# Slot order of the first attention: scores two tiles ahead, exponential ahead of the FiLM copies, weight folding last on TensorE

## The chip, the cores and the metric

The kernel runs on one core of a Trainium2 chip. The metric is the device time of one execution in microseconds (us), lower is better. The engines are TensorE (PE, with PEld for its weight loads), VectorE (DVE), ScalarE (ACT), GpSimd (POOL) and SyncE (SP, which here only issues DMAs). Each engine runs its own instruction stream in order; engines meet at semaphores.

## The reference, cut to what matters

The whole program is two layers, each an attention and a mixture of experts; the change is confined to the first attention and to the work that is run beside it. For every token the first attention keeps the 32 largest of 64 scores per head, takes a softmax over them, averages over four heads, and makes from the result a scale and a shift (FiLM) for the normalised token:

```python
Q = (x_text @ Wq).reshape(Bb, Tt, H, DH)
K = (x_vision @ Wk).reshape(Bb, Gg, H, DH)
scores = jnp.einsum('bthd,bghd->bhtg', Q, K) / np.sqrt(DH)
topv, topi = jax.lax.top_k(scores, K_TOP)          # 32 of 64
probs = jax.nn.softmax(topv, axis=-1)
attn_mean = attn.mean(axis=1)                      # over the 4 heads
c_t = jnp.einsum('btg,bgd->btd', attn_mean, V)
scale_in, shift_in = jnp.split(c_t @ W_film_in + b_film_in, 2, axis=-1)
x = x * (1.0 + mod_gate * scale_in) + mod_gate * shift_in
y = s4d(x, log_dt, A_re, A_im, C_re, C_im, D_skip)
```

Two things that later stages need are made in the same stage: the convolution kernel of `s4d` (powers of complex numbers, then a Toeplitz layout in memory), and the expert weights of the last stage with their low-rank parts added (`W + A B`, transposed; called folding).

## The kernel before

The stage `first_attention` (L596 on) works on 32 tiles of 128 tokens. Every engine runs a loop of slots, `march(slot, first, last)`; in slot x each engine handles several tiles at different depths, `x.by(d)` being tile x+d. Nothing but the order of the code and the semaphores sets the order of the work. Buffers are doubled by the tile's parity (`j`).

For tile x the chain is as follows. PE turns the token and context rows (`turn`, L815 and L818), ACT copies them from PSUM (`xf`, `cf`). PE projects queries and keys (`qk`, L833 and L834), ACT copies them (`qt`, and four copies into `kb`). PE makes the scores into `pss` (L808), ACT copies them into `dd`, POOL adds the mask term and writes `sc` (L741). DVE selects in four rounds of four MAX8 (L937) and four MATCH_REPLACE8 (L950). After the first round POOL writes `sc` minus the maximum into `dd` (L737), ACT takes the exponential `ee` (L895). In the next slot DVE makes the masked product `pr` out of `work` and `ee` (L958), its sum and reciprocal (`weights`). POOL scales and adds up the heads into `at` (L748 to L754). PE turns `at` (L839), ACT copies it into the block-diagonal `abd`, PE multiplies it with the context (`vec`, L829, the wait names say u), ACT copies `us`, PE makes the FiLM rows (`film`, L825), ACT copies them (`fi`, `FO`), and POOL applies them (L759 to L762).

Beside this runs a list of 34 pieces, one a slot (`side_job`): PE makes piece x+3 in slot x (`side_piece`) into the one PSUM bank `side`, and ACT copies piece x+2 out of it in slot x (`keep_piece`). PE starts piece n only when ACT has kept piece n-1 (`side_kept`). From piece 13 on they come in threes for each expert: turn (one transpose), first (eight matmul pairs, L281 and L283), second (four pairs, L293 and L294). Piece 7 is first of expert 0 and piece 12 its second. The folded weights stand in one buffer, `fold.done`, that SP stores to memory after each second; ACT's copy of the next first waits for that store.

The order within a slot before is, on PE: score of tile x+1, turn x+3, film x-3, vec x-2, qk x+2, side piece, turn of `at` x-1. On ACT: score copy x+1, turn copies x+3, `us` x-2, kept piece, normalised tile, exponential x, `qt` and `kb` x+2, FiLM copies x-3, `abd` x-1. POOL has, besides its part of the chain, products of complex powers in slots 1 to 4 (`kernel_part`, K.more of 4 at once in slot 4), `fold_norm` in slot 0 and the second normalisation of eight tiles in every eighth slot.

Of the kernel before, what the change touches and what calls it, by code (L numbers as in the profile page):

```python
# [11 lines left out]
ALU = mybir.AluOpType  # L12
# [3 lines left out]
P = 128  # L16
# [198 lines left out]
class Fold:  # L215
# [9 lines left out]
    def __init__(self, C, A, G, ctx):  # L225
        self.A, self.G = A, G
        NC = self.NC

        def sb(name, shape, n):
            return [C.sb(f"fold_{name}{j}", shape, ctx=ctx) for j in range(n)]  # L230

        self.wr, self.w2r = sb("wr", [P, 2, NC, D], self.DEPTH), sb("w2r", [D, HE], self.DEPTH)
        self.br, self.b2r = (C.sb("fold_" + n, [P, NE, k], ctx=ctx) for n, k in (("br", P), ("b2r", 32)))
        self.ar, self.a2 = C.sb("fold_ar", [P, NE, D], ctx=ctx), C.sb("fold_a2", [P, NE // 4, HE], ctx=ctx)
        self.bt, self.bt2 = sb("bt", [P, P], 2), C.sb("fold_bt2", [P, NE // 4, P], ctx=ctx)
        self.done = C.sb("fold_done", [P, 2 * NC * P + NC * D], ctx=ctx)

    def semaphores(self, C):
        self.factors, self.added, self.stored = (C.sem("fold_" + n) for n in ("factors", "added", "stored"))
        self.loaded = [C.sem(f"fold_loaded{j}") for j in range(self.DEPTH)]  # L240
# [22 lines left out]
    def store(self, sp, e):  # L263
        sp.dma_start(self.G.folded[e, :, 0:2 * self.NC * P + self.NC * D], self.done[:]).then_inc(self.stored, 16)
# [38 lines left out]
    def keep_first(self, act, bank, e):  # L303
        after(act, self.stored, 16 * e)
        return act.activation(self.done[:, 0:2 * self.NC * P], bank[:, 0:2 * self.NC * P], ACT.Copy)

    def keep_weights(self, act, bank, e):
        n = 2 * self.NC * P
        return act.activation(self.done[:, n:n + self.NC * D], bank[:, 0:self.NC * D], ACT.Copy)
# [12 lines left out]
class Kernel:  # L322
# [263 lines left out]
def first_attention(nc, C, A, G):  # L586
# [4 lines left out]
    with ExitStack() as ctx:  # L591
        def two(name, shape):
# [5 lines left out]
        sc, wk_, m8 = two("sc", [P, H0, T]), two("work", [P, H0, T]), two("m8", [P, H0, 4, 8])  # L598
        dd, ee, pr = two("dd", [P, H0, T]), two("ee", [P, H0, T]), two("pr", [P, H0, T])
# [11 lines left out]
            "turned", "turned_sb", "qk", "qk_sb", "scores", "scores_kept", "scores_sb", "max", "diff", "exp",  # L611
# [25 lines left out]
        with nc.Block() as block:  # L637
# [5 lines left out]
            def _(sp):  # L643
# [31 lines left out]
                march(slot, -3, NT + 2)  # L675
                sp.wait_ge(s["toeplitz"], 16 * 4)
                sp.wait_ge(fold.stored, 16 * NE)

            @block.gpsimd
            def _(pool):  # L680
# [17 lines left out]
                def kernel_part(t):  # L698

                    U, z1 = K.U, K.one(K.V, 1)  # L700
                    if t == 1:
                        step.then(pool.tensor_scalar(K.t[:, 0, :], z1[0], -1.0, None, ALU.add))
                        K.times(step, pool, K.one(U, 0), (K.t[:, 0, :], z1[1]), K.Q, K.tu)
                    if t == 2:
                        pool.wait_ge(s["powers"], 2)
                        K.more(step, pool, U, 1, K.z[8], K.tu)
                    if t == 3:
                        K.more(step, pool, U, 2, K.z[16], K.tu)
# [20 lines left out]
                def slot(x):  # L729
                    j, a, c, m, n = x.j, x.by(3), x.by(-4), x.by(-1), x.by(1)  # L730
                    if x.t == 0:
                        fold_norm()
                    if x.real() and x.t % 8 == 0:
                        second_norm(slice(x.t, x.t + 8))
# [4 lines left out]
                    if n.real():  # L739
                        pool.wait_ge(s["scores_kept"], n.t + 1)  # L740
                        pool.tensor_tensor(sc[n.j][:], dd[n.j][:], wide(G.pen[:, n.t:n.t + 1, :], [P, H0, T]),  # L741
                                           ALU.add).then_inc(s["scores_sb"], 1)
                        pool.wait_ge(s["scores_sb"], n.t + 1)
# [19 lines left out]
                    if c.real():  # L763
                        pool.wait_ge(s["mod"], c.t + 1)
                    kernel_part(x.t)

                march(slot, -3, NT + 4)

            @block.tensor
            def _(pe):  # L770
                def side_piece(n):
                    name, e = side_job(n)
# [28 lines left out]
                def slot(x):  # L801
                    turn, qk, score, attn, vec, film = (x.by(d) for d in (3, 2, 1, -1, -2, -3))
# [38 lines left out]
                march(slot, -3, NT + 3)  # L841

            @block.scalar
            def _(act):
# [30 lines left out]
                def slot(x):  # L875
                    turn, qk, attn, vec, film, score, n = (x.by(d) for d in (3, 2, -1, -2, -3, 1, KEPT))
                    if score.real():
                        act.wait_ge(s["scores"], score.t + 1)
                        copy(dd[score.j][:].rearrange("p h g -> p (h g)"), pss[score.j][:, 0:H0 * T]).then_inc(s["scores_kept"], 1)
                    if turn.real():  # L880
# [4 lines left out]
                        copy(cf[j][:], psa[j][0:DC, P:2 * P]).then_inc(s["turned_sb"], 1)  # L885
                    if vec.real():
                        act.wait_ge(s["u"], vec.t + 1)
                        copy(us[vec.j][0:DC, :], psb[vec.j][0:DC, P:2 * P]).then_inc(s["u_sb"], 1)
                    keep_piece(x.t + 2)
                    if x.real() and n.real():  # L890
                        act.activation(G.XT[:, n.t, :], G.X[:, n.t, :], ACT.Identity, scale=norm["rstd"][:, n.t:n.t + 1],
                                       bias=norm["shift"][:, n.t:n.t + 1]).then_inc(s["normal"], 1)
                    if x.real():
                        act.wait_ge(s["diff"], x.t + 1)
                        act.activation(ee[x.j][:], dd[x.j][:], ACT.Exp, scale=scale).then_inc(s["exp"], 1)  # L895
# [9 lines left out]
                    if film.real():  # L905
                        act.wait_ge(s["film"], film.t + 1)
                        after(act, s["mod"], film.t - 1)
                        copy(fi[film.j][:], psf[:, 0:256])
                        copy(G.FO[:, film.t, :], psf[:, 256:512]).then_inc(s["film_sb"], 1)
# [6 lines left out]
                march(slot, -3, NT + 3)  # L916

            @block.vector
            def _(dve):
# [11 lines left out]
                def top(x, r, src, ready):  # L931

                    marks = []
                    for h in range(H0):
                        if r > 0:
                            own.wait(ready[h])
# [7 lines left out]
                def replace(x, r, src, h, found):  # L944
# [5 lines left out]
                    return own.did(dve.match_replace(wk_[x.j][:, h, :], m8[x.j][:, h, r, :], src[:, h, :], TAKEN))  # L950
# [1634 lines left out]
```

## Time and profile before

| | |
|---|---|
| time, median of three runs (lowest, highest) | 938.17 us (937.61, 940.75) |
| span of the profiled execution | 935.4 us |
| busy share of the span: PE, DVE, ACT, POOL | 76%, 72%, 51%, 60% |
| first attention, from the first MAX8 to the last masked product | 33.04 to 247.75 us |
| DVE waiting for the exponential in it | 21.0 us in 12 waits |
| mean granted TensorE clock from 94 to 248 us | 0.74 of full speed |

The profile is of one execution; its span is from the first to the last instruction. The granted clock is the share of full speed at which TensorE was allowed to run; 1.00 and 0.50 are its two levels of 2.4 and 1.2 GHz. A timeline row gives the start, the duration, the engine, the line of the kernel, the operation and its operands, and in square brackets the idle time of the engine just ahead of it with what ended it.

### The profile page before, as it was taken

What the parts mean: (1) busy time and instruction counts of PE and PEld (TensorE: products, weight loads), DVE (VectorE), ACT (ScalarE), POOL (GpSimd) and SP (SyncE); (2) the same over time, 40 slices, a digit from 0 to 9 for tenths busy, and PEclk for the clock granted to TensorE, in tenths of its full rate; (3) what the DMA queues carried; (4) which work ended last, traced back from release to release, by engine and by line L of the source; (5) the groups of instructions that cost most, each with busy time, mean ns of one, the idle gap of its engine ahead of it and who ended that gap; (6) DMA issues with size and microseconds to landing.
All of it is one profiled execution on the core that took longest, in us unless ns stands there. A gap on an engine that the chain in (4) does not pass through costs nothing. (4 is left out here: it accounts for less than half of the span.)

```text
span 935.4 us, 20537 instructions
## 1 busy us (share of the span) xinstructions
PE 710.3 (76%) x6072; PEld 508.4 (54%) x6072; DVE 673.2 (72%) x3212; ACT 473.4 (51%) x1318; POOL 564.8 (60%) x931
## 2 busy tenths in 40 slices
PE   0686898979883999972498528998888874799970
PEld 0353554545483656631275426766666652699970
DVE  6898989978524688769111167598998887699974
ACT  3566576735200455450133175577777761577740
POOL 7688877766526544210677667345777767277770
PEclk9767787957555999996599855798988885899995
DMA  6300112997213977700365330000000002698928
GB/s 143 57 25 10 41 45 64 86 88 96 40 45 140 290 250 257 243 23 0 39 115 132 88 137 1 2 4 13 25 26 25 25 28 76 216 279 264 260 69 270
DMA packets 98829, 94.41 MB, mean 101 GB/s; under 512 B 37511, under 2 KB 82302, under 8 KB 98142
## 3 DMA queue, kind: packets, MB, share of 16 engines
q1 hardware_dynamic: 91268, 79.34, 33.1%
q0 software_dynamic: 6592, 13.58, 6.0%
q8 instruction: 50, 0.82, 0.4%
q14 instruction: 61, 0.50, 0.3%
q10 hardware_dynamic: 858, 0.17, 0.1%
HBM read 47.76 MB, written 43.19 MB: 97 GB/s over the span
## 5 line engine op out<-in xcount | busy, mean ns | idle before, releaser
L2402 POOL DMA_INDIRECT expert_pairs<-e_ys,e_home x78 | 75.4, 967 | 38.4 <-issue 23.5
L1742 POOL TENSOR_SCALAR a_kb<-a_kr,a_m,a_bk 128x128 f32<-128x128 f32 x128 | 57.9, 452 | 44.4 <-ACT a_kr L1981 32.3
L1760 POOL DMA_INDIRECT expert_slots<-r_rows,r_slotu x64 | 63.3, 989 | 30.3 <-DVE r_rows L2136 15.1
L950 DVE MATCH_REPLACE8 work<-m,work 128x64 f32<-128x64 f32 x384 | 75.7, 207 | 0.0
L1484 POOL DMA_INDIRECT ex_rows<-rows,slot_source x32 | 30.7, 960 | 52.7 <-POOLq L1163 43.2
L937 DVE MAX8 m<-work 128x8 f32<-128x64 f32 x384 | 57.0, 209 | 0.0
L825 PE MATMUL psf<-filmw,us 97*128 97x512 f32 x64 | 51.6, 902 | 3.0 <-ACT FO L846 2.9
L1815 PE MATMUL a_pss<-a_kb,a_qt 32*64 32x256 f32 x512 | 41.5, 463 | 13.9 <-ACT a_pp L1966 11.7
L2168 DVE TENSOR_REDUCE a_mx<-a_pss 128x8 f32<-128x512 f32 x64 | 43.9, 686 | 8.1 <-PE a_pss L1815 7.8
L2369 PE MATMUL e_ps<-e_XH,e_wh 128*128 128x256 f32 x156 | 48.1, 308 | 1.5 <-DVE e_XL L2414 1.5
L1536 ACT ACTIVATE ex_hs<-ex_psh,vec 128x512 f32<-128x512 f32 x32 | 22.0, 687 | 51.2 <-PE ex_psh L1517 50.5
L2371 PE MATMUL e_ps<-e_XH,e_wl 128*128 128x256 f32 x156 | 44.6, 286 | 0.0
L2370 PE MATMUL e_ps<-e_XL,e_wh 128*128 128x256 f32 x156 | 44.6, 286 | 0.0
L1961 ACT ACTIVATE a_pp<-a_dd 128x512 f32<-128x512 f32 x32 | 20.2, 631 | 45.1 <-DVE a_dd L2177 45.1
L1890 PE MATMUL a_psp<-ident,a_pp 128*128 128x128 f32 x256 | 39.5, 306 | 1.9 <-ACT a_pt L2014 1.9
L2219 DVE RECIPROCAL a_rt<-a_pso 128x128 f32<-128x128 f32 x31 | 29.5, 951 | 14.8 <-PE a_pso L1882 11.9
L1309 ACT ACTIVATE rt_rs<-mlp_psh,vec 128x512 f32<-128x512 f32 x32 | 22.0, 687 | 34.7 <-PE mlp_psh L1267 34.7
L203 POOL TENSOR_SCALAR mlp_ln_v<-mlp_ln_mv 128x4 f32<-128x4 f32 x24 | 5.5, 229 | 54.0 <-DVE mlp_ln_mv L195 54.0
L1494 POOL DMA_INDIRECT planes<-ex_ys,slot_home x32 | 31.2, 976 | 10.9 <-issue 9.1
L2177 DVE TENSOR_TENSOR a_dd<-a_mx,a_pss 128x512 f32<-128x512 f32 x64 | 35.5, 554 | 2.2
L808 PE MATMUL pss<-kb,qt 128*64 128x256 f32 x128 | 28.9, 541 | 10.7 <-ACT kb L846 10.7
L2014 ACT ACTIVATE a_pt<-a_psp 128x512 f32<-128x512 f32 x64 | 35.4, 611 | 2.2 <-PE a_psp L1890 2.0
(464 smaller groups left out, 2418.2 us busy)
## 6 DMA issues: line engine op xcount, KB each, us to landing
expert_slots<-rt_unfilled SPq DMA_DIRECT2D x151, 130.0 KB, 2.6
ahead<-folded_weights SPq DMA_DIRECT2D x20, 386.0 KB
e_wf<-folded_weights SPq DMA_DIRECT2D x19, 386.0 KB, 4.2
planes<-rt_zeros SPq DMA_DIRECT2D x4, 1024.0 KB
ew<-in_L_ffn_ew SPq DMA_DIRECT2D x16, 256.0 KB, 4.0
pair_y<-expert_pairs SPq DMA_DIRECT2D x16, 256.0 KB, 5.6
e_xr<-expert_slots SPq DMA_DIRECT2D x27, 130.0 KB, 3.3
folded_weights<-fold_done SPq DMA_DIRECT2D x8, 384.0 KB, 4.3
```

The lines of the kernel that those rows point to most:

```text
L825: pe.matmul(psf[:], us[j][:], G.filmw[:], start=True, stop=True).then_inc(s["film"], 1)
L937: mx = dve.max(m8[x.j][:, h, r, :], src[:, h, :])
L950: return own.did(dve.match_replace(wk_[x.j][:, h, :], m8[x.j][:, h, r, :], src[:, h, :], TAKEN))
L1742: m = pool.tensor_scalar(kb[a.j][:, :, h, :], k, m4[:, h:h + 1], bk4[:, h:h + 1], ALU.mult, ALU.add)
L1760: pool.indirect_dma_start(G.slots, bass.IndirectOffsetOnAxis(ap=slot[:, b, k, t:t + 1], axis=0), rb[b % NB][:, k, t, :], None).then_inc(se ...
L1815: mm = pe.matmul(pss[half][T * b:T * b + T, h, 0:HG * T], qt[g.j][rows, T * b:T * b + T], kb[g.j][rows, b, :, :], start=True, stop=True)
L1890: mm = pe.transpose(psp[half][:, k, :], pp[x.j][:, h:h + 2, :].rearrange("p h k -> p (h k)"), G.ident[:])
L2168: dve.tensor_reduce(m, scores(half), AX.X, ALU.min).then_inc(s["lowest"], 1)
L2369: pe.matmul(psh[m][c][:], wh[j][:, m, c, :], XH[j][:], start=True, stop=False)
L2370: pe.matmul(psh[m][c][:], wh[j][:, m, c, :], XL[j][:], start=False, stop=False)
L2371: pe.matmul(psh[m][c][:], wl[j][:, m, c, :], XH[j][:], start=False, stop=True).then_inc(h_ps[m][c], 1)
L2402: pool.indirect_dma_start(G.pair, bass.IndirectOffsetOnAxis(ap=home[i % NY][:, k:k + 1], axis=0), ys[i % NY][:, k, :], None).then_inc(kept ...
```

## The change

On PE every tile is turned, projected and scored one slot earlier than before (turn x+4, qk x+3, score x+2), and the side piece moves from ahead of the turn of `at` to the end of the slot. ACT's order becomes: score copy x+2 (into a buffer of its own, `raw`), turn copies x+4, exponential x, FiLM copies x-3, `us` x-2, `qt` and `kb` x+3, kept piece, normalised tile, `abd` x-1. POOL adds the mask two tiles ahead, and for that waits until DVE has read the buffer it writes over (`replaced`, a new semaphore, which the last MATCH_REPLACE8 of the first round raises). `fold.done` is doubled, with one store semaphore for each half. POOL's products start two slots earlier, the largest is split over slots 2 and 3, `fold_norm` moves to the end of slot 1, and the second normalisation is split into four tiles in each of two slots. SP's loop starts at slot -2 and not at -3, its order within a slot is as before.

```diff
     def keep_first(self, act, bank, e):
-        after(act, self.stored, 16 * e)
-        return act.activation(self.done[:, 0:2 * self.NC * P], bank[:, 0:2 * self.NC * P], ACT.Copy)
+        after(act, self.stored[e % 2], 16 * (e // 2))
+        return act.activation(self.done[e % 2][:, 0:2 * self.NC * P], bank[:, 0:2 * self.NC * P], ACT.Copy)
...
+    def half_of_more(self, step, eng, z, a, factor, room, part):
+        by = tuple(wide(q.unsqueeze(1), [P, a, NS]) for q in factor)
+        u, out = self.powers(z, 0, a), self.powers(z, a, a)[part]
+        t0, t1 = (room[:, k, 0:a, :] for k in range(2))
+        eng.tensor_tensor(t0, u[0], by[part], ALU.mult)
+        step.then(eng.tensor_tensor(t1, u[1], by[1 - part], ALU.mult))
+        step.then(eng.tensor_tensor(out, t0, t1, ALU.add if part else ALU.subtract))
...
-                march(slot, -3, NT + 2)
+                march(slot, -2, NT + 2)
...
-                    if t == 4:
-                        K.more(step, pool, U, 4, K.z[32], K.tu)
+                    if t in (2, 3):
+                        K.half_of_more(step, pool, U, 4, K.z[32], K.tu, t - 2)
...
-                    j, a, c, m, n = x.j, x.by(3), x.by(-4), x.by(-1), x.by(1)
+                    j, a, c, m, n = x.j, x.by(4), x.by(-4), x.by(-1), x.by(2)
...
-                        pool.tensor_tensor(sc[n.j][:], dd[n.j][:], wide(G.pen[:, n.t:n.t + 1, :], [P, H0, T]),
+                        if x.real():
+                            pool.wait_ge(s["replaced"], x.t + 1)
+                            pool.wait_ge(s["diff"], x.t + 1)
+                        pool.tensor_tensor(sc[n.j][:], raw[n.j][:], wide(G.pen[:, n.t:n.t + 1, :], [P, H0, T]),
...
-                    turn, qk, score, attn, vec, film = (x.by(d) for d in (3, 2, 1, -1, -2, -3))
+                    turn, qk, score, attn, vec, film = (x.by(d) for d in (4, 3, 2, -1, -2, -3))
...
-                    side_piece(x.t + 3)
                     if attn.real():
                         pe.wait_ge(s["attn"], attn.t + 1)
                         after(pe, s["u_sb"], attn.t - 1)
                         pe.transpose(psb[attn.j][:, 0:P], at[attn.j][:], G.ident[:]).then_inc(s["attn_turned"], 1)
+                    side_piece(x.t + 3)
```

ACT in one slot of the middle of the stage, before (from the score copy on; `fold_done` is the kept side piece, here a first):

```order
L846 ACTIVATE dd<-pss 128x256 [waits att0_scores]
L846 ACTIVATE xf<-psa 128x128 [waits att0_ctx_kept,att0_turned]
L846 ACTIVATE cf<-psa 96x128
L846 ACTIVATE us<-psb 96x128 [waits att0_u]
L305 ACTIVATE fold_done<-side 128x512 [waits fold_stored,att0_side]
L891 ACTIVATE XT<-X,FO 128x128
L895 ACTIVATE ee<-dd 128x256 [waits att0_diff]
L846 ACTIVATE qt<-psa 128x128 [waits att0_scores,att0_qk]
L846 ACTIVATE kb<-psa 32x2x64 x4
L846 ACTIVATE fi<-psf 128x256 [waits att0_mod,att0_film]
L846 ACTIVATE FO<-psf 128x256
```

The same slot of ACT now:

```order
L861 ACTIVATE raw<-pss 128x256 [waits att0_scores_sb,att0_scores]
L861 ACTIVATE xf<-psa 128x128 [waits att0_ctx_kept,att0_turned]
L861 ACTIVATE cf<-psa 96x128
L904 ACTIVATE ee<-dd 128x256 [waits att0_diff]
L861 ACTIVATE fi<-psf 128x256 [waits att0_mod,att0_film]
L861 ACTIVATE FO<-psf 128x256
L861 ACTIVATE us<-psb 96x128 [waits att0_u]
L861 ACTIVATE qt<-psa 128x128 [waits att0_scores,att0_qk]
L861 ACTIVATE kb<-psa 32x2x64 x4
L306 ACTIVATE fold_done<-side 128x512 [waits fold_stored0,att0_side]
```

The exponential moved from behind `us` and the kept piece to right behind the turn copies; the kept piece moved from ahead of the exponential to behind `qt` and `kb`.

PE at the end of a slot and the start of the next, before (L273 is the side piece, a turn; L839 turns `at`; L808 opens the next slot):

```order
L833 MATMUL psa<-xf,wq 128x128 [waits att0_turned_sb]
L834 MATMUL psa<-cf,wk 128x128
L273 MATMUL side<-ident,fold_br 128x128 [waits att0_side_kept]
L839 MATMUL psb<-ident,at 128x128 [waits att0_u_sb,att0_attn]
L808 MATMUL pss<-kb,qt 64x256 [waits att0_scores_kept,att0_qk_sb]
```

The same place of PE now:

```order
L848 MATMUL psa<-xf,wq 128x128 [waits att0_turned_sb]
L849 MATMUL psa<-cf,wk 128x128
L853 MATMUL psb<-ident,at 128x128 [waits att0_u_sb,att0_attn]
L274 MATMUL side<-ident,fold_br 128x128 [waits att0_side_kept]
L823 MATMUL pss<-kb,qt 64x256 [waits att0_scores_kept,att0_qk_sb]
```

The side piece stands between the turn of `at` and the next slot's scores, with the same wait for the kept piece as before.

## Rows read from the trace of the kernel before

**Rows 1.** The page's first line.
```profile
span 935.4 us, 20537 instructions
```

**Rows 2.** Waits, 34 to 250 us: us in total, times, longest.
```profile
ACT us L846 <- PE psb L829: 35.8, 29, 2.0
...
DVE pr L958 <- ACT ee L895: 21.0, 12, 3.6
```

**Rows 3.** Timeline of DVE: the masked products of tiles 0, 9, 10, 24, 30.
```profile
40.50 0.48 DVE L958 SCALAR_TENSOR_TENSOR pr<-work,ee 128x256 f32<-128x256 f32 x1 [2.25 <-ACT ee L895]
...
99.58 0.43 DVE L958 SCALAR_TENSOR_TENSOR pr<-work,ee 128x256 f32<-128x256 f32 x1
...
105.66 0.68 DVE L958 SCALAR_TENSOR_TENSOR pr<-work,ee 128x256 f32<-128x256 f32 x1
...
198.58 0.43 DVE L958 SCALAR_TENSOR_TENSOR pr<-work,ee 128x256 f32<-128x256 f32 x1 [3.55 <-ACT ee L895]
...
241.62 0.43 DVE L958 SCALAR_TENSOR_TENSOR pr<-work,ee 128x256 f32<-128x256 f32 x1 [2.10 <-ACT ee L895]
```

**Rows 4.** Timeline, PE and ACT in one slot at clock 1.00.
```profile
177.06 0.65 PE L808 MATMUL pss<-kb,qt 128*64 128x256 f32 x4
...
178.39 0.27 ACT L846 ACTIVATE cf<-psa 96x128 f32<-96x128 f32 x1
...
179.22 0.39 PE L834 MATMUL psa<-cf,wk 96*128 96x128 f32 x2
...
180.02 0.41 ACT L895 ACTIVATE ee<-dd 128x256 f32<-128x256 f32 x1
...
180.48 1.09 ACT L846 ACTIVATE kb<-psa 32x128 f32<-32x128 f32 x4
...
181.60 0.38 ACT L846 ACTIVATE fi<-psf 128x256 f32<-128x256 f32 x1
...
181.88 0.38 ACT L846 ACTIVATE FO<-psf 128x256 f32<-128x256 f32 x1
```

**Rows 5.** Timeline, PE and ACT in one slot at clock 0.50.
```profile
201.59 1.12 PE L808 MATMUL pss<-kb,qt 128*64 128x256 f32 x4
...
205.50 0.27 ACT L846 ACTIVATE us<-psb 96x128 f32<-96x128 f32 x1 [1.70 <-PE psb L829]
...
205.68 0.63 PE L834 MATMUL psa<-cf,wk 96*128 96x128 f32 x2
...
205.94 0.41 ACT L895 ACTIVATE ee<-dd 128x256 f32<-128x256 f32 x1
...
207.67 1.12 PE L808 MATMUL pss<-kb,qt 128*64 128x256 f32 x4 [0.89 <-ACT kb L846]
```

**Rows 6.** Timeline of PE: a first from beginning to end at clock 1.00, then 0.50.
```profile
184.26 0.49 PE L281 MATMUL side<-ident,fold_wr 128*128 128x128 f32 x2
...
187.59 0.47 PE L839 MATMUL psb<-ident,at 128*128 128x128 f32 x1
...
230.86 0.68 PE L281 MATMUL side<-ident,fold_wr 128*128 128x128 f32 x2
...
236.52 0.47 PE L839 MATMUL psb<-ident,at 128*128 128x128 f32 x1
```

**Rows 7.** Windows: length, busy PE, PEld, DVE, ACT, POOL, then clock, DMA share, GB/s.
```profile
94.00:248.00 154.00, 132.57 (x511) 78.81 (x511) 137.16 (x1173) 90.05 (x343) 110.41 (x240) 0.74 0.54 67
...
104.00:106.00 2.00, 0.00 (x0) 0.00 (x0) 1.87 (x16) 1.94 (x8) 1.76 (x4) 0.90 0.00 1
```

**Rows 8.** Timeline of ACT: the kept first that waited for a store.
```profile
197.64 0.60 ACT L305 ACTIVATE fold_done<-side 128x512 f32<-128x512 f32 x1 [5.47 <-DMA folded_weights<-fold_done]
```

**Rows 9.** Timeline of POOL: K.more in slot 4, its first instruction and what follows its six.
```profile
66.37 0.72 POOL L314 TENSOR_TENSOR toe<-toe 128x256 f32<-128x256 f32 x1
...
71.05 0.62 POOL L737 TENSOR_TENSOR dd<-sc,m 128x256 f32<-128x256 f32 x1 [0.18 <-POOL toe L319]
```

**Rows 10.** Instructions on the context rows `cs`: time from issue to landing of their loads.
```profile
DMA to landing us min/median/max: 1.7/1.8/14.8
```

More of the change, by code:

```diff
@@ L263, in store @@
     def store(self, sp, e):
-        sp.dma_start(self.G.folded[e, :, 0:2 * self.NC * P + self.NC * D], self.done[:]).then_inc(self.stored, 16)
+        sp.dma_start(self.G.folded[e, :, 0:2 * self.NC * P + self.NC * D], self.done[e % 2][:]).then_inc(self.stored[e % 2], 16)
     def turn_second(self, pe, bank):
@@ L762, in slot @@
                         pool.tensor_tensor(G.XM[:, c.t, :], xn[:], fi[c.j][:, D:2 * D], ALU.add).then_inc(s["mod"], 1)
-                    if c.real():
                         pool.wait_ge(s["mod"], c.t + 1)
                     kernel_part(x.t)
-                march(slot, -3, NT + 4)
+                    if x.t == 1:
+                        fold_norm()
+                    if x.real() and x.t % 8 in (0, 1):
+                        at_once = 8 * (x.t // 8) + 4 * (x.t % 8)
+                        second_norm(slice(at_once, at_once + 4))
+                march(slot, -4, NT + 4)
             @block.tensor
@@ L875, in slot @@
                 def slot(x):
-                    turn, qk, attn, vec, film, score, n = (x.by(d) for d in (3, 2, -1, -2, -3, 1, KEPT))
+                    turn, qk, attn, vec, film, score, n = (x.by(d) for d in (4, 3, -1, -2, -3, 2, KEPT))
                     if score.real():
                         act.wait_ge(s["scores"], score.t + 1)
-                        copy(dd[score.j][:].rearrange("p h g -> p (h g)"), pss[score.j][:, 0:H0 * T]).then_inc(s["scores_kept"], 1)
+                        after(act, s["scores_sb"], score.t - 1)
+                        copy(raw[score.j][:].rearrange("p h g -> p (h g)"), pss[score.j][:, 0:H0 * T]).then_inc(s["scores_kept"], 1)
                     if turn.real():
@@ L885, in slot @@
                         copy(cf[j][:], psa[j][0:DC, P:2 * P]).then_inc(s["turned_sb"], 1)
+                    if x.real():
+                        act.wait_ge(s["diff"], x.t + 1)
+                        act.activation(ee[x.j][:], dd[x.j][:], ACT.Exp, scale=scale).then_inc(s["exp"], 1)
+                    if film.real():
+                        act.wait_ge(s["film"], film.t + 1)
+                        after(act, s["mod"], film.t - 1)
+                        copy(fi[film.j][:], psf[:, 0:256])
+                        copy(G.FO[:, film.t, :], psf[:, 256:512]).then_inc(s["film_sb"], 1)
                     if vec.real():
@@ L904, in slot @@
                         m.then_inc(s["qk_sb"], 1)
[L905 to L909, printed above, removed]
+                    keep_piece(x.t + 2)
+                    if x.real() and n.real():
+                        act.activation(G.XT[:, n.t, :], G.X[:, n.t, :], ACT.Identity, scale=norm["rstd"][:, n.t:n.t + 1],
+                                       bias=norm["shift"][:, n.t:n.t + 1]).then_inc(s["normal"], 1)
                     if attn.real():
@@ L934, in top @@
                     for h in range(H0):
-                        if r > 0:
+                        if r == 1 and h == H0 - 1:
+                            dve.wait_ge(s["replaced"], x.t + 1)
+                        elif r > 0:
                             own.wait(ready[h])
@@ L949, in replace @@
                         own.wait(found[h])
-                    return own.did(dve.match_replace(wk_[x.j][:, h, :], m8[x.j][:, h, r, :], src[:, h, :], TAKEN))
+                    taken = dve.match_replace(wk_[x.j][:, h, :], m8[x.j][:, h, r, :], src[:, h, :], TAKEN)
+                    if r == 0 and h == H0 - 1:
+                        taken.then_inc(s["replaced"], 1)
+                        return None
+                    return own.did(taken)
                 def slot(x):
```

38 lines of the change are left out of this document (15 added, 23 removed).

## The prediction, made before the changed kernel was run

> **What bounds the kernel now.** I read the page's first line for the size of the whole: a span of 935.4 us [rows 1], 2.8 us below the median of the three runs, 938.17 us. I add the change that I work out for the span to that median. Only the first attention is touched, so every term is a difference inside its 215 us. I read the waits of that stage next, then DVE's timeline, then PE and ACT side by side in a slot at either clock.
>
> DVE sets the pace where nothing goes wrong. Its masked product comes once in a slot, and from tile 9 to tile 10 that takes 6.08 us [rows 3] with no wait. From tile 9 to tile 30 it takes 142.04 us for 21 slots, where 21 x 6.08 = 127.7, so 14.4 us are lost there. Nearly all that DVE waits for in the stage is the exponential, 21.0 us in 12 waits [rows 2].
>
> The exponential is late because ACT stands in front of it: ACT waits 35.8 us for PE's vec product to copy `us` [rows 2], and the kept piece and the exponential stand behind that copy. At clock 0.50 the exponential starts 205.94 - 201.59 = 4.35 us after PE began the slot's scores [rows 5]. Behind that is PE itself. At clock 0.50 its fixed part, from the scores to the end of the key projection, is 206.31 - 201.59 = 4.72 us [rows 5]; at 1.00 it is 179.61 - 177.06 = 2.55 us [rows 4]. A first adds 5.66 or 3.33 us [rows 6]. A second has half as many pairs: 2.83 or 1.67 us. A turn is one transpose like that of `at`: 0.47 us at the low clock [rows 6], and by my estimate half of that, 0.24, at the high one.
>
> So three slots (turn, first, second), which I call a round, cost DVE 18.24 us. They cost PE at clock 1.00 3 x (2.55 + 0.24) + 0.24 + 3.33 + 1.67 = 13.6 us. At 0.50 a slot with a turn takes 6.08 us [rows 5], held by `kb`; one with a first 4.72 + 0.47 + 5.66 = 10.85; one with a second 8.02; together 24.95. PE is far ahead at one clock and far behind at the other. The granted clock over 94 to 248 us is 0.74 [rows 7], which is (1 - 0.74) / 0.5 = 52% of the time at the low level. If PE's lead at the high clock were of no use later, a round would take 1 / (0.48/18.24 + 0.52/24.95) = 21.2 us; if all of it were, DVE's 18.24. Measured: 142.04 / 7 = 20.3. The two loops together thus explain the pace before, and I use the same form for the kernel after.
>
> **The change, part by part.**
>
> *The exponential ahead.* It now needs PE's scores and turns alone, not film, vec, `us` and the kept piece. At clock 1.00 the turn copies end at 178.39 + 0.27, 1.6 us after the slot's scores began [rows 4]. At 0.50 I estimate 2.2 us: the scores and transposes double, the two copies don't. Against 4.35 [rows 5], PE may fall some 2.2 us further behind before DVE waits. That is a margin, spent once as long as PE does not win it back.
>
> *Weight folding last.* The bank `side` holds one piece: PE makes piece x+3 when ACT has kept piece x+2. ACT did that right behind `us`, about when PE ended its key projection, so PE hardly waited. Now the kept piece stands behind the exponential, both FiLM copies, `us`, `qt` and four `kb` copies. The `at` transpose that PE does meanwhile covers 0.24 to 0.47 us of this. And behind the piece waits the next slot, since scores, turns, exponential and FiLM of slot x+1 all come after piece x+3 on PE. This closes a loop: scores, ACT's whole chain, kept piece, side piece, next scores.
>
> Its length at clock 1.00, from the start of the scores: 1.6 for the turn copies; 0.46 for exponential and `qt` (180.02 to 180.48); 0.28 + 0.38 for FiLM; 0.27 for `us` [rows 5]; 1.09 for `kb` [rows 4]; and the kept piece, 0.60 for a first [rows 8] and like the copies of 128 and 256 columns, 0.27 and 0.38 [rows 4], for the others, 0.42 on average. That sums to 4.50 us. The copies overlap by about 0.1 at each seam (`FO` starts 0.28 after `fi`, which lasts 0.38), which makes 4.0 at the least; I take 4.25. At 0.50 the key projection ends later than ACT's queue: 4.72 + 0.2 for `qt` + 1.09 + 0.42 = 6.45 us with the signal.
>
> A round of this loop is 3 x 4.25 + 5.24 = 18.0 us at clock 1.00, no shorter than DVE's 18.24: PE can no longer win anything back. At 0.50 it is 3 x 6.45 + 0.47 + 5.66 + 2.83 = 28.3, against 24.95. With 52% at the low clock a round takes 1 / (0.48/18.24 + 0.52/28.3) = 22.4 us.
>
> *Two buffers for the folded weights.* Once, a kept first waited 5.47 us for a store [rows 8], and DVE lost 3.55 us behind it [rows 3]. That is inside the 142.04 us, and goes. PE stood still through it at the low clock; I count it as two points of the share: 50%, a round of 1 / (0.50/18.24 + 0.50/28.3) = 22.2 us. Seven rounds are 155.3, that is 13.3 more than 142.04; less the margin of 2.2, **+11 us**.
>
> *POOL.* It is busy 110.41 us in the 25 slots between 94 and 248 us [rows 7], 4.4 of 6.08 each. The wait for `replaced` lies inside the 1.7 us that are left; nothing but POOL's own part stands behind it, and the masked scores are two tiles ahead. Cost: none, at most 1 us in the stage. In the start, tile 0's wait of 2.25 us [rows 3] goes, because `fold_norm` and the normalisation no longer stand ahead of its difference. The product of slot 4, six instructions that hold POOL for 71.05 - 66.37 = 4.7 us [rows 9], is split. But slot 1 now carries a product of half that width (2.3 to 4.7 us), `fold_norm` and four tiles' normalisation on top of its own work, and DVE may wait some 2.5 us for tile 2's exponential. Between -4 and +3 us, I take 0.
>
> *Context rows.* PE turns tile x+4, and SP issues the load of x+6 when vec of x-2 is done, as before. A load now has two slots, some 12 us, where it had three. The median landing takes 1.8 us, the longest 14.8 [rows 10], so between 0 and 3 us once; I take 0. The Toeplitz rows and stores behind it on SP's queue keep their order. Scores two tiles ahead buy nothing themselves: the only wait of DVE of any size is the exponential [rows 2].
>
> Sum: 938.2 + 11 = **949 us**.
>
> **The rivals.**
>
> *Faster: the exponential was all.* If the side loop is hidden, DVE runs at 6.08 throughout: 14.4 us of the 21 slots and 2.25 of the start go, 921.5 us. The 12 waits for the exponential speak for it, and that the whole ACT chain fits into 6.08 us at clock 1.00. It needs the high clock: the loop after equals the pace before (20.3, with the margin 20.6) at a low-clock share of 32%, and below that the change wins. The removed stand of 5.5 us at the low clock speaks for a lower share. Between 920 and 935 us.
>
> *No change.* Gain and longer loop cancel, at 25 to 37% low clock and with the start a little better: 935.5 to 941. That the exponential moves in name only, because it still waits behind PE's scores and turns, which come behind the side piece, ends here too.
>
> *Clearly slower: the clock falls.* In the loop PE stands idle in every slot, at 0.50 for 6.45 - 4.72 - 0.47 = 1.3 us and at 1.00 for about 1.4. Idle does cost clock here: PE has no instruction from 104 to 106 us, and the mean clock of that stretch is already 0.90 [rows 7], on the way from 1.00 to 0.50. With 75% of the time low a round takes 1 / (0.25/18.24 + 0.75/28.3) = 24.9 us: 174.1 for seven, +32 less 2 is 968 us. Against it: PE stood still for as long in slots before, where it waited for `at`. The Trainium skill speaks for this rival, "TensorE: Matmul & The Clock Gate", section "A second HAM failure mode: psum-queue depth-cycling": where TensorE pauses between groups of matmuls because it hands PSUM banks round, its clock swings and throughput falls even if the matmuls themselves are fast. The one bank `side` is such a hand-over; the row at 104 agrees that a pause costs clock, and no row shows yet what a pause in every slot does.
>
> **How the numbers follow.** The forecast (a low-clock share of about 40 to 62%, 941 to 960 us) gets 0.50, the fallen clock (beyond 960) 0.18, no change 0.14, faster 0.18. A measurement of this kernel can tell about 0.3%, 2.8 us, from no change. So faster is 0.18, same 0.14, slower 0.68. The range takes in the share from 75%, 968 us, down into the upper part of the faster case; the bounds of the start and of the loads lie inside. 930 to 968 leaves out about 0.1 on either side.
>
> **What will show it.** Right: PE waits for ACT's kept piece ahead of nearly every side piece (hardly any before), the round at clock 1.00 is near 18 us and at 0.50 near 28, the wait of ACT for `us` shrinks while DVE's wait for the exponential grows, most after a first at the low clock, and the wait for the store is gone. Wrong: slots of 6.08 us through the low clock, or PE's waits ahead of the side piece below 0.5 us. A mean clock above 0.84 in the stage would make it faster, one below 0.65 slower than the forecast. A POOL busy without a pause over several slots after slot 10 would refute its zero.

## The result and the profile after

The changed kernel takes **989.09 us** (median of four runs, 984.53 to 990.42) where the kernel before takes 938.89 beside it: a ratio of 1.0548, 95% interval 1.0501 to 1.0595, some 50 us slower. The forecast was 949 us with a range up to 968. The direction was right; the size was that of the third rival, "clearly slower: the clock falls", which had a chance of 0.18, and it went 21 us beyond that rival's price of 968. Where one execution of a kernel below ran far slower than its others at a clearly lower granted clock, its median is that of the others.

The page of the kernel after: first line, busy times, and the granted clock in 40 slices (each about 25 us, so the first attention is the slices 2 to 12).

```profile
span 989.2 us, 20586 instructions
...
PE 746.6 (75%) x6072; PEld 530.6 (54%) x6072; DVE 673.1 (68%) x3212; ACT 474.9 (48%) x1318; POOL 571.1 (58%) x947
...
PEclk9967765565555579999659975589988886799995
```

The span is 53.8 us above that of [rows 1], and the first attention holds nearly all of it. DVE's masked products, the marks of [rows 3], show where. These are the products of tiles 0, 9, 10 and 30, and between the last two those that bound three slots at the low clock: one with a first (149.47 to 161.65), one with a second (241.26 to 250.86) and one with a turn (250.86 to 257.76):

```profile
41.46 0.67 DVE L980 SCALAR_TENSOR_TENSOR pr<-work,ee 128x256 f32<-128x256 f32 x1 [3.01 <-ACT ee L904]
...
108.79 0.69 DVE L980 SCALAR_TENSOR_TENSOR pr<-work,ee 128x256 f32<-128x256 f32 x1 [0.71 <-ACT ee L904]
...
118.28 0.70 DVE L980 SCALAR_TENSOR_TENSOR pr<-work,ee 128x256 f32<-128x256 f32 x1 [3.28 <-ACT ee L904]
...
149.47 0.42 DVE L980 SCALAR_TENSOR_TENSOR pr<-work,ee 128x256 f32<-128x256 f32 x1 [0.95 <-ACT ee L904]
...
161.65 0.42 DVE L980 SCALAR_TENSOR_TENSOR pr<-work,ee 128x256 f32<-128x256 f32 x1 [6.23 <-ACT ee L904]
...
241.26 0.43 DVE L980 SCALAR_TENSOR_TENSOR pr<-work,ee 128x256 f32<-128x256 f32 x1 [4.96 <-ACT ee L904]
...
250.86 0.43 DVE L980 SCALAR_TENSOR_TENSOR pr<-work,ee 128x256 f32<-128x256 f32 x1 [3.66 <-ACT ee L904]
...
257.76 0.44 DVE L980 SCALAR_TENSOR_TENSOR pr<-work,ee 128x256 f32<-128x256 f32 x1 [0.96 <-ACT ee L904]
...
290.54 0.56 DVE L980 SCALAR_TENSOR_TENSOR pr<-work,ee 128x256 f32<-128x256 f32 x1
```

From tile 0 to tile 9 the stage now takes 67.33 us where it took 59.08; with tile 0 itself 0.96 later, tile 9 is 9.2 us late. From tile 9 to tile 30 it takes 181.75 us where it took 142.04, which is 39.7 more. Together tile 30 is 48.9 us late. The waits of the stage (34 to 310 us; us in total, times, longest) name the loop of the prediction:

```profile
ACT raw L861 <- PE pss L823: 83.3, 31, 6.3
POOL sc L753 <- ACT raw L861: 77.3, 22, 7.1
DVE pr L980 <- ACT ee L904: 71.0, 25, 6.2
...
PE psb L853 <- POOL at L765: 20.3, 15, 6.3
...
PE side L294 <- ACT fold_done L306: 10.5, 7, 1.8
PE side L274 <- ACT fold_done L310: 9.1, 6, 1.6
...
PE side L282 <- ACT fold_bt L302: 5.7, 6, 1.4
```

ACT no longer waits for PE's vec product [rows 2] but for PE's scores, 83.3 us: the whole slot begins late. DVE's wait for the exponential went from 21.0 us in 12 [rows 2] to 71.0 in 25. PE waits for the kept piece ahead of its side piece, 25.3 us in 19 waits, 1.33 each, about the 1.3 of the prediction. In the kernel before (34 to 250 us) it waited 8.5 us in 11 there, 5.6 of them in the one wait for the store:

```profile
PE side L293 <- ACT fold_done L305: 7.4, 5, 5.6
...
PE side L273 <- ACT fold_done L309: 1.1, 6, 0.2
```

The clock is the other part. Three windows of the kernel after: tile 0 to tile 9, tile 9 to tile 30, and 23 us inside it (length; busy PE, PEld, DVE, ACT, POOL; granted clock, DMA share, GB/s). Behind them are the same two stretches of the kernel before.

```profile
41.40:108.80 67.40, 46.19 (x180) 27.57 (x179) 54.33 (x460) 38.83 (x136) 50.84 (x108) 0.75 0.05 12
108.80:290.50 181.70, 149.03 (x463) 87.97 (x463) 125.97 (x1071) 84.34 (x318) 107.86 (x234) 0.59 0.39 57
139.00:162.00 23.00, 20.01 (x59) 11.67 (x59) 13.19 (x114) 9.52 (x36) 10.45 (x23) 0.50 0.15 41
```

```profile
40.50:99.60 59.10, 45.84 (x181) 27.07 (x181) 54.05 (x460) 38.76 (x139) 51.48 (x111) 0.68 0.06 15
99.60:241.60 142.00, 121.68 (x479) 72.43 (x479) 125.51 (x1071) 84.70 (x323) 100.73 (x218) 0.75 0.58 73
```

0.59 is (1 - 0.59) / 0.5 = 82% of the time at the low level, where the kernel before had a granted clock of 0.75, or 50%, between the same two tiles. From 139 to 162 us PE stays at the low level throughout.

### The profile page after: what moved, and what is told of

Read it like the earlier page. It is cut to its first block and busy times, and to the rows that moved or that the text cites. A ratio compares the mean times of both kernels' runs of the same rounds, so it can differ in the third digit from the quotient of the medians.

```text
span 989.2 us, 20586 instructions
## 1 busy us (share of the span) xinstructions
PE 746.6 (75%) x6072; PEld 530.6 (54%) x6072; DVE 673.1 (68%) x3212; ACT 474.9 (48%) x1318; POOL 571.1 (58%) x947
## 5 line engine op out<-in xcount | busy, mean ns | idle before, releaser
L753 POOL TENSOR_TENSOR sc<-raw,pen 128x256 f32<-128x256 f32 x32 | 23.1, 723 | 79.5 <-ACT raw L861 78.0
L980 DVE SCALAR_TENSOR_TENSOR pr<-work,ee 128x256 f32<-128x256 f32 x32 | 15.8, 494 | 71.9 <-ACT ee L904 71.0
L840 PE MATMUL psf<-filmw,us 97*128 97x512 f32 x64 | 59.7, 1034 | 1.0 <-ACT us L861 1.0
L861 ACT ACTIVATE raw<-pss 128x256 f32<-128x256 f32 x32 | 12.3, 383 | 84.5 <-PE pss L823 84.5
```

Source lines behind the costliest of these rows:

```text
L840: pe.matmul(psf[:], us[j][:], G.filmw[:], start=True, stop=True).then_inc(s["film"], 1)
```

## The experiments

The theory was: the kept piece behind ACT's whole queue and the one bank `side` close a loop through PE and ACT; PE pauses in it in every slot; and the granted clock falls with that, which makes each turn of the loop longer. The rivals were that one of the other parts (POOL's split work, the wait for `replaced`, the context loads, the exponential's new place) costs the time, and that the loop alone does so without the clock.

### The two moves of the side piece, undone one by one

The kept piece goes back to the front of ACT's queue, here right behind the exponential:

```diff
                     if x.real():
                         ... exponential ...
+                    keep_piece(x.t + 2)
                     if film.real():
...
-                    keep_piece(x.t + 2)
```

> The changed kernel with one move undone: ScalarE's copy of the side piece stands right behind the exponential again, ahead of the FiLM copies, us, qt and kb; TensorE keeps the side piece last. Theory of the side loop (the piece is kept too late, and TensorE stands in front of the bank): the wait ahead of the side pieces goes, a round (turn, first, second) at clock 0.50 falls from 27.4-28 to about 25, at 1.00 it is about 19 because the turn of at waits for POOL; 960 to 970 us. Rival, the clock fell for another reason and ScalarE's order does not matter: 985 to 990 us. Rival, TensorE's order (folding last) is to blame: 985 or more.

Measured: 951.72 us in two runs, ratio 1.0118 (1.0083 to 1.0153), which is less than any of the expectations. One line on ACT gives back 37 of the 50 us. No wait for the kept piece ahead of a side piece is left; PE now waits longer for `at`. Waits from 34 to 300 us, and the window from tile 9 to tile 30:

```profile
PE psb L853 <- POOL at L765: 38.4, 18, 6.0
...
DVE pr L980 <- ACT ee L904: 36.4, 15, 4.7
```

```profile
102.10:257.90 155.80, 136.50 (x469) 84.35 (x470) 126.79 (x1071) 85.49 (x319) 108.52 (x236) 0.62 0.52 66
```

The 13 us that stay belong to PE's other move, as the kernel with both moves back shows below: with the side piece behind the turn of `at`, PE has nothing to do while it waits for `at`. The clock is still at 0.62, yet the stretch is 26 us shorter than in the kernel after, at 0.59: a low clock without the late kept piece costs far less. How much of the 13 us is the clock is not shown.

The other move alone, the side piece back ahead of the turn of `at`, the kept piece still last on ACT:

```diff
+                    side_piece(x.t + 3)
                     if attn.real():
                         ... turn of at ...
-                    side_piece(x.t + 3)
```

> The changed kernel with TensorE's part undone alone: the side piece stands ahead of the turn of at again; ScalarE keeps its new order. Theory of the side loop: the piece still waits for the late copy, and the turn of at (0.33 to 0.42 us) no longer lies in that wait but is added to the loop: 990 to 1000 us. Rival, folding last in TensorE's slot is to blame: 940 to 955 us.

Measured: 995.92 us in two runs, 1.0588 (1.0553 to 1.0623), 7 us slower than the kernel after, as the theory had it. Nothing covers the wait for the kept piece any more: its three lines sum to 36.7 us in 21 (34 to 300 us), against 25.3 in 19. So it is the place on ACT that costs, and behind it PE's move softens the loss.

```profile
PE side L274 <- ACT fold_done L310: 12.6, 7, 2.0
PE side L282 <- ACT fold_bt L302: 12.3, 8, 1.7
PE side L294 <- ACT fold_done L306: 11.8, 6, 2.0
```

Both moves back, all else of the change kept:

> The changed kernel with both moves undone: kept piece right behind the exponential, side piece ahead of the turn of at. What is left of the change: scores two tiles ahead, the exponential early, two buffers, POOL's new order. Theory of the side loop: a round at 0.50 is back at about 25, at 1.00 DVE sets 18.2, and the early exponential gains what the change was meant to gain: 920 to 938 us. Rival, the early start or POOL's new order costs by itself: 945 us or more, with the loss in the first ten slots.

Measured: 938.62 us in ten runs, 0.9989 (0.9964 to 1.0013); the gain that the theory expected (920 to 938) did not come. Thus the two moves of the side piece hold the whole loss, and all other parts of the change come to nothing together. The window from tile 9 to tile 30 stands at a clock of 0.71:

```profile
101.10:247.30 146.20, 124.05 (x470) 74.98 (x471) 128.18 (x1071) 84.14 (x319) 107.15 (x236) 0.71 0.59 71
```

The nothing is itself a balance, and the trace shows its losing side. In slot 1, POOL's `fold_norm` (from L737) and four tiles' normalisation stand ahead of tile 2's difference, which comes 3.57 us after `fold_norm` began, and DVE waits 3.98 us. In slot 9 a Toeplitz product of 2.35 us comes on top of the other four tiles' normalisation, and DVE waits 3.28 us at tile 10. Both waits are in the kernel after too, 3.01 us at tile 2 and 3.28 at tile 10 (the row at 118.28). And PE waits 5.33 us for a load of context rows. Timelines of POOL, ACT and DVE at tile 2, of POOL and DVE at tile 10, and of PE, in the kernel with both moves back:

```profile
49.66 0.46 POOL L737 TENSOR_TENSOR xn<-filmw,bin 97x128 f32<-97x128 f32 x1
...
53.23 0.62 POOL L746 TENSOR_TENSOR dd<-sc,m 128x256 f32<-128x256 f32 x1
...
53.88 0.42 ACT L904 ACTIVATE ee<-dd 128x256 f32<-128x256 f32 x1 [4.70 <-POOL dd L746]
54.33 0.69 DVE L980 SCALAR_TENSOR_TENSOR pr<-work,ee 128x256 f32<-128x256 f32 x1 [3.98 <-ACT ee L904]
...
105.08 2.35 POOL L731 TENSOR_TENSOR toe<-toe 128x1024 f32<-128x1024 f32 x1
...
110.47 0.69 DVE L980 SCALAR_TENSOR_TENSOR pr<-work,ee 128x256 f32<-128x256 f32 x1 [3.28 <-ACT ee L904]
```

```profile
191.07 0.45 PE L833 MATMUL psa<-ident,cs 128*96 128x128 f32 x1 [5.33 <-DMA cs<-in_ctx]
```

### Is it the one bank?

The kernel after with two banks for the side piece, PE waiting for one kept piece less, except ahead of a first and of two early pieces, `film` and `sums` (the second bank came from laying both score tiles into one):

```diff
-        pss = [C.ps(f"pss{j}", [P, 512], ctx) for j in range(2)]
+        pss_both = C.ps("pss", [P, 512], ctx)
+        pss = [pss_both[:, 256 * j:256 * j + 256] for j in range(2)]
-        side = C.ps("side", [P, 512], ctx)
+        sides = [C.ps(f"side{j}", [P, 512], ctx) for j in range(2)]
...
-                    after(pe, s["side_kept"], n)
+                    after(pe, s["side_kept"], n if name in ("film", "sums", "first") else n - 1)
+                    side = sides[n % 2]
```

> The changed kernel with its orders as they are, but two PSUM banks for the side pieces (the two score buffers share a bank): a turn and a second no longer wait for the copy of the piece before; a first still does, since it reads that copy. Theory of the side loop: two of three waits go, a round at 0.50 falls by about 2.5 us to 25, 970 to 980 us. Rival, the bank is not what TensorE waits for: 985 to 990 us.

Measured: 956.19 us in two runs, 1.0165 (1.0125 to 1.0206), better than the 970 to 980 of the theory. The kept piece stands where the change put it, and 33 of the 50 us go all the same: the hand-over of the bank is the loop. In the window the clock is back at 0.73, and PE's wait for `at` is again the longest that is left on PE (45.7 us in 22, 34 to 300 us). From tile 9 to tile 30 it takes the same 156 us as the kernel with the kept piece alone put back, which ran at 0.62: between these two kernels the higher clock did not go with a shorter stretch.

```profile
105.00:260.60 155.60, 126.66 (x469) 76.86 (x470) 127.48 (x1071) 83.53 (x318) 108.59 (x236) 0.73 0.56 67
```

### Is it the clock?

The kernel after with one more matmul in each slot, ahead of the wait for `at`, into a half of the bank that nobody reads. It adds work to PE and takes none away (the wait for `us` moves ahead of it):

```diff
                     if attn.real():
+                        after(pe, s["u_sb"], attn.t - 1)
+                        pe.matmul(psb[attn.j][:, 256:512], G.wq[:], G.X[:, 0:2, :], start=True, stop=True)
                         pe.wait_ge(s["attn"], attn.t + 1)
-                        after(pe, s["u_sb"], attn.t - 1)
```

> The changed kernel with one more matmul of 128x256 in every slot ahead of the turn of at, written where nobody reads, inside the time in which TensorE waits for the kept piece (1.3 us at 0.50, the matmul takes about 0.85 there). Theory of the clock: the standing in every slot is what keeps the clock low; the low share after tile 9 falls from 78% towards 50%, 960 to 975 us. Rival: the loop alone sets the pace, the clock doesn't move: 987 to 995 us.

Measured: 958.39 us in two runs, 1.0231 (1.0165 to 1.0297): 31 us **less** than the kernel after, with more work. The order of the loop is untouched, its pauses are filled in part, and the clock rises from 0.59 to 0.80 between tile 9 and tile 30. The waits of PE for the kept piece shrink with it (10.5 to 5.2 us ahead of the seconds), and DVE waits 39.0 us for the exponential and not 71.0; a turn of the loop is shorter at the high clock (4.23 us against 6.70, in the rows of the next section). PE still waits 30.0 us for `at`. The window, and that wait:

```profile
105.60:258.90 153.30, 126.81 (x506) 76.05 (x506) 125.97 (x1072) 83.83 (x318) 108.98 (x236) 0.80 0.52 68
```

```profile
DVE pr L981 <- ACT ee L905: 39.0, 22, 3.7
```

It stays slower than the kernel with both moves back, which takes 146.2 us for the same tiles at a *lower* clock, 0.71. So the new order costs by itself too, and the clock multiplies it.

### The part that the change was thought to win by

The kernel before with the exponential right behind the turn copies on ACT, and `fold_norm` at the end of slot 1 on POOL, nothing else. What the exponential overtakes are `us` and the kept piece; ahead of the FiLM copies it stood in the kernel before as well:

```diff
+                    if x.real():
+                        act.wait_ge(s["diff"], x.t + 1)
+                        act.activation(ee[x.j][:], dd[x.j][:], ACT.Exp, scale=scale).then_inc(s["exp"], 1)
                     if vec.real():
...
-                    if x.t == 0:
-                        fold_norm()
...
+                    if x.t == 1:
+                        fold_norm()
```

> The kernel before with one part of the change alone: the exponential stands right behind the turn copies on ScalarE, ahead of us and the kept piece (with POOL's fold_norm moved to the end of slot 1, without which the order would lock up). Theory: the loop through the side bank stays as short as before, and most of the 14.4 us that DVE lost to the exponential after tile 9 goes: 922 to 933 us. Rival: the exponential was only the last link, and DVE waits as long for TensorE's scores and turns in front of it: 936 to 940 us.

Measured: 935.39 us in ten runs (926.61 to 939.75), 0.9969 (0.9929 to 1.0009): no difference that can be told, and between the two expectations. Tile 0 is 2.2 us earlier (38.30 for 40.50), the wait of [rows 3] that the prediction gave back to the start. But from tile 9 to tile 30 it takes 141.91 us, as before. The one buffer of the folded weights is still there, ACT waits 7.8 us for two stores, and DVE 15.7 us in 8 for the exponential, 5.76 of them behind the longer store: the exponential's place alone, with one buffer, does not win the 14.4 us that the first rival built on.

### What the remaining parts cost

Both moves back, with ten buffers for the context rows and not eight, and SP's loop from slot -4:

```diff
-RING = 8
+RING = 10
...
-                march(slot, -2, NT + 2)
+                march(slot, -4, NT + 2)
```

> The kernel with both moves undone (both_back), with ten buffers for the context rows in place of eight and the loads issued two tiles earlier. Theory: the 5.3 us that TensorE waited there for one load at about 186 us go, and with them DVE's waits right behind (4.4 and 0.7 us): 3 to 5 us below both_back, 933 to 936 us. Rival: that wait is covered, within 1 us of both_back.

Measured: 930.72 us in three runs (922.37 to 930.80), 0.9891 (0.9814 to 0.9968), about 8 us below the kernel with both moves back (the intervals just touch), where 3 to 5 were expected. No wait of PE for a load is left, and from tile 9 to tile 30 it takes 138.6 us for 146.2, one execution of each. The shorter lead of the loads had a price once the loop was out of the way; that it was as much as 8 us is not certain.

On top of that, POOL's products one slot earlier each, and the second normalisation in the slots 3 and 4 of each eight and not in 0 and 1:

```diff
-                    if t in (2, 3):
-                        K.half_of_more(step, pool, U, 4, K.z[32], K.tu, t - 2)
+                    if t in (1, 2):
+                        K.half_of_more(step, pool, U, 4, K.z[32], K.tu, t - 1)
...
-                    if x.real() and x.t % 8 in (0, 1):
-                        at_once = 8 * (x.t // 8) + 4 * (x.t % 8)
+                    if x.real() and x.t % 8 in (3, 4):
+                        at_once = 8 * (x.t // 8) + 4 * (x.t % 8 - 3)
```

> ring10 with POOL's extra work spread: the complex products one slot earlier still, the second normalisation of four tiles in slots 3 and 4 of every eight and not in 0 and 1. Theory: DVE's waits at tile 2 (3.0 us in ring10) and tile 10 (3.3 us) come from POOL's overfull slots 1 and 9 and go: 4 to 6 us below ring10's 930.8, 925 to 928 us. Rival: those slots are late for TensorE's sake: 930 to 932 us.

Measured: 927.84 us in eleven runs (921.26 to 933.93), 0.9923 (0.9882 to 0.9964). The intervals of this kernel and the last overlap widely, so the time settles nothing between them; the trace shows which waits went. The waits of DVE at tiles 2 and 10 are gone, its wait for the exponential is 6.5 us in 3, and tile 30 comes at 232.95 where it came at 236.84.

The same with the unread matmul, and the kernel before with it:

> spread with the matmul of 128x256 in every slot ahead of the turn of at. Theory of the clock: the added work raises the granted clock here too, but TensorE has little standing left to fill at 0.50, where the matmul lengthens the loop by 0.85 us a slot: within 5 us of spread. Rival: the clock is what still costs, and 10 us or more go.

> The kernel before with the matmul of 128x256 in every slot ahead of the turn of at. If the clock is worth as much there as in the changed kernel, the low share (52%) falls by a third and 5 to 10 us go: 928 to 933 us. If TensorE has no standing to fill, the matmul costs 0.85 us in each slot at 0.50, some 15 slots: 940 to 950 us.

Measured: 921.63 us (921.34 to 922.43), 0.9868 (0.9811 to 0.9924), for the first. That is the lowest median of all, below both the kernel before and the kernel after. It is 6.2 us below the kernel without the matmul, between what theory and rival expected; the intervals of the two overlap, and their traces differ by 3.7 us between tile 9 and tile 30 (132.45 for 136.13), so that the size of this last gain is not certain. The kernel before with the matmul: 933.41 us in ten runs (928.26 to 940.24), 0.9996 (0.9957 to 1.0035), no difference that can be told, and between the two expectations. Windows from 94 to 240 us, the first kernel and then the second:

```profile
94.00:240.00 146.00, 126.93 (x541) 77.00 (x541) 138.32 (x1150) 86.90 (x334) 114.13 (x254) 0.85 0.67 72
```

```profile
94.00:240.00 146.00, 129.61 (x537) 77.48 (x538) 127.86 (x1090) 87.32 (x331) 104.85 (x226) 0.82 0.53 65
```

The clock rose in both. In the kernel before it gave nothing that can be told: in the traced execution (939.88 us, one of its slowest) the exponential still stands in ACT's queue behind the kept piece, a kept first waits for a store (6.9 us in two), and DVE waits 24.5 us for the exponential. In the other, DVE waits 0.8 us for it in the whole stage. This fits that a faster PE pays only where PE is what comes last; no run isolates it.

## Why the prediction was wrong, and what in it was right

**The loop** was right, to its length. At the low level, from the scores of one slot to the next side piece, 6.45 us were forecast; the timeline of PE and ACT after reads 245.41 - 238.71 = 6.70, with the exponential 2.10 us behind the scores (2.2 forecast):

```profile
238.71 1.12 PE L823 MATMUL pss<-kb,qt 128*64 128x256 f32 x4
...
240.81 0.41 ACT L904 ACTIVATE ee<-dd 128x256 f32<-128x256 f32 x1
...
242.80 0.63 PE L849 MATMUL psa<-cf,wk 96*128 96x128 f32 x2
...
243.64 1.09 ACT L861 ACTIVATE kb<-psa 32x128 f32<-32x128 f32 x4
...
244.76 0.60 ACT L306 ACTIVATE fold_done<-side 128x512 f32<-128x512 f32 x1
...
245.41 0.80 PE L294 MATMUL side<-ident,fold_w2r 128*128 128x128 f32 x2 [1.76 <-ACT fold_done L306]
...
248.31 1.12 PE L823 MATMUL pss<-kb,qt 128*64 128x256 f32 x4
```

A reader sees the loop in one piece: kept piece at the end of ACT's queue, PE idle for 1.76 us, only then the side piece, a second, and behind it the next scores, 9.60 us after the last ones (8.02 was the price of such a slot before). DVE's rows bear out each kind of slot where the clock is 0.50 throughout: 6.90 us with a turn (257.76 - 250.86), 12.18 with a first (161.65 - 149.47) and 9.60 with a second (250.86 - 241.26), 28.7 in all for a forecast of 28.3 and 24.95 before. At the high level, 4.25 us were forecast, and it is 206.20 - 201.97 = 4.23:

```profile
201.97 0.65 PE L823 MATMUL pss<-kb,qt 128*64 128x256 f32 x4
...
204.75 1.10 ACT L861 ACTIVATE kb<-psa 32x128 f32<-32x128 f32 x4
...
205.75 0.33 PE L853 MATMUL psb<-ident,at 128*128 128x128 f32 x1 [1.23 <-POOL at L765]
205.87 0.28 ACT L302 ACTIVATE fold_bt<-side 128x128 f32<-128x128 f32 x1
206.20 0.49 PE L282 MATMUL side<-ident,fold_wr 128*128 128x128 f32 x2
```

Here PE waits 1.23 us for `at`, and the kept piece ends (205.87 + 0.28) right where the side piece begins: the loop closes on time, with a second wait inside it that the prediction had not placed there.

**The low-clock share is the step that failed.** "With 52% at the low clock", less two points for the removed store wait, was the share of the kernel before carried over to another kernel. Measured: 82%. Put into the prediction's own form, 1 / (0.18/18.24 + 0.82/28.3) = 25.7 us for a round; seven make 180.2, and 181.75 were measured. So by that form the longer loop at the old share is the 13.3 us that the prediction had, and the fall of the share another 24.9, of the 39.7 that the 21 slots lost. The kernel with the unread matmul speaks for the size: 28.5 us less for these slots (153.28) at 40% low, where the form gives 31. The experiments show that the two parts do not simply add up. Against 146.2 us with both moves back, the change's order at a clock of 0.80 costs 7 us (153.3), a clock of 0.62 without the late kept piece 10 (155.8), and both together 36: most of the loss needs the long loop and the low clock at once. And 3.28 of the 39.7 are tile 10's, which POOL's slot 9 costs with both moves back too. The prediction had the mechanism before it and gave it 0.18, with 75% for its share. Its argument against it, that PE stood as long before where it waited for `at`, overlooked that the change leaves those pauses and adds others: in the stage after, PE waits 20.3 us for `at` (15.4 before) *and* 25.3 for the kept piece. Of the two signs that it named, the one on the clock came true: a mean below 0.65, and slower than the forecast.

The Trainium skill spoke for that rival ("TensorE: Matmul & The Clock Gate", section "A second HAM failure mode: psum-queue depth-cycling": pauses between groups of matmuls, from handing PSUM banks round, make the clock swing and cost throughput though each matmul is fast). The trace now agrees, with 0.59 where it had 0.75. The clock swings here too (1.00 from 202 to 206 us), but it also stayed at 0.50 from 139 to 162 us on end.

**The margin** of 2.2 us that the earlier exponential was to give back is not to be seen in the slots: with it the form would give 178.0, and without it 180.2, for 181.75.

**The first ten slots** were taken as 0 (-4 to +3) and cost 9.2. The prediction put the loop on the 21 slots after tile 9 alone, though side pieces are kept in the first ten too, and PE waits for them. With both moves back tile 9 comes at 101.1 us, so 7.7 of the 9.2 belong to the two moves of the side piece; a lower clock cannot be the reason, since it was 0.75 from tile 0 to tile 9 after and 0.68 before. The other 1.5 is what the rest of the start costs on balance: with both moves back tile 0 is 2.26 earlier, and tile 2's wait, forecast as "some 2.5 us", is 3.98.

**POOL's zero** was half right. The wait for `replaced` costs nothing in the kernel after, as forecast: no line of POOL's waits names it (with both moves back, 1.8 us in 4). But "nothing but POOL's own part stands behind it" was wrong: on POOL the mask two tiles ahead stands before the `at` of the slot, and it waits for ACT's copy of PE's scores (77.3 us in 22; before, the mask one tile ahead stood in the same place and waited 19.3 us in 10). So `at` comes late whenever the scores do, and PE then waits for `at`, as in the slot at the high level above. And POOL is overfull in slot 9, for 3.28 us of DVE's time, in the kernel after and with both moves back; that lies outside its 0 to 1.

**The context loads**, 0 to 3 us once and taken as 0, cost nothing in the kernel after: no line of PE's waits there names a load. With both moves back, PE waits 5.33 us for one, and ten buffers bring about 8 us (930.72 for 938.62). There the bound was too low.

**The store wait** went, as forecast: no line of ACT's waits after names a store. **The other rivals**: "the exponential was all" fell with the kernel that has it almost alone (0.9969); "no change" fell with the result.

**The estimate** of 0.24 us for a turn at the high clock is 0.33 in the row at 205.75; 0.09 us in a slot changes no conclusion.

What stays open is how much of the loss in slots at the low level would be left if PE's pauses for `at` alone, or for the kept piece alone, were filled: the unread matmul stands ahead of `at`, and fills a part of either.

## What to carry to other kernels

Where two engines hand one PSUM bank back and forth, follow the bank through both in-order queues before you move either end: moving the copy that frees it to the back of one queue makes all that stands ahead of it part of the loop. The granted clock of the stretch before is no input for the kernel after: count the places where TensorE will wait in every slot, and work the sum out at both ends of the clock, not at the old mean. And when a change comes out at nothing, undo it by parts; here a gain in the start, a late load and two overfull slots of GpSimd cancelled, and with the losses removed and part of PE's waits filled, the median was 921.63 us.

## What the runs showed of the hardware

One matmul more per slot, of 128 x 256 with a result that nobody reads, put where TensorE waits anyway, raised the granted clock between tile 9 and tile 30 from 0.59 to 0.80 and took 31 us off the kernel after. It did the same to the clock of the kernel before (0.75 to 0.82 from 94 to 240 us) with no gain in time that can be told, and in the version without the late load and the overfull slots the median went from 927.84 to 921.63 us, with intervals that overlap. And a higher clock does not by itself mean a shorter stretch: from tile 0 to tile 9 the kernel after ran at 0.75 and took 67.3 us, the kernel before at 0.68 and took 59.1.
